# A chunked delta-rule stage: the state update taken over all 128 rows, the output products set directly behind it, and like weight shapes set side by side at the end of a pair

## The chip, the cores and the metric

The kernel is one launch on one core of a Trainium2 chip. The metric is the device time of that launch in microseconds (us). The program is deterministic in what it issues: each engine has its own instruction queue, written out by hand, and the queues meet only in semaphores.

## The reference, cut to what matters

Four layers follow each other on 8 sequences of 512 rows of width 256: attention, a feed-forward layer with 4-bit weights, a gated delta rule, and a feed-forward layer with ternary weights. The change is in the third. Its core is a scan over chunks of 64 rows, with a 128x128 state S for each head (8 heads, 8 chunks in a sequence):

```python
def step(S, inp):
    q_i, k_i, v_i, kc_i, g_i, dm_i = inp
    attn = jnp.where(keep_low, q_i @ jnp.swapaxes(k_i, -1, -2) * dm_i, 0.0)
    v_n = v_i - kc_i @ S
    out = q_i * jnp.exp(g_i)[..., None] @ S + attn @ v_n
    g_last = g_i[..., -1]
    S = S * jnp.exp(g_last)[..., None, None] + jnp.einsum('bhck,bhcv->bhkv',
            k_i * jnp.exp(g_last[..., None] - g_i)[..., None], v_n)
    return (S, out)
```

Ahead of the scan each head needs its projections (q, k, v and an output gate z from one weight matrix), a convolution of four taps, norms, and the inverse of a 64x64 triangular matrix for each chunk (`solve_triangular`). All of it is in float32.

## The kernel before, in words

`delta_rule` is the third stage, between 1061 and some 2940 us of the profiled execution. It works on pairs of heads: 8 sequences of 4 pairs make `PAIRS` = 32 pairs, and `e` is 0 or 1 for the head in the pair. A tile `t` is 128 rows of the sequence (`TPS` = 4) and holds `CPT` = 2 chunks of `CK` = 64 rows; a chunk `m` (`NCH` = 8) has `t = m // 2`, `c = m % 2`, and lies in the partitions `rows(c)`, which are 0 to 63 or 64 to 127.

Every engine runs `for q in range(-1, PAIRS)` with two pairs in hand: the scan of pair `q` (the back) and the projections, taps and norms of pair `f = q + 1` (the front). The first part of a turn is a loop over `n` from 0 to 8, in which step `n` of the scan is mixed with pieces of the front (`front_early(f, n)`, `front_late(f, n)`) in an order written by hand. Then come `LEVELS` - 1 = 5 levels of the triangular inverse for pair `f` and, last, products that prepare its scan. I call the loop over `n` the loop, and the products after the levels the end of the pair.

A step `n` of the scan is a chain between TensorE (PE) and VectorE (DVE), for both heads one after the other:

- PE, line 1966: one product of `PQ` with the state `S` gives k_cum times S and q times S (`p1_mm`)
- DVE, line 1743: `V2`, the new values of the chunk, 64 partitions (`w_done`); ScalarE (ACT), line 1493: the half of the output that comes from S (`o1_done`)
- PE, line 1982: the state update, `KK` transposed times `V2`, over the 64 partitions of the chunk (`ds_mm`)
- DVE, line 1759: `S` is scaled and the update is added (`s_done`), after which PE can start step n + 1

At every odd `n` a tile is complete: PE forms the output products `AT` times `V2` (line 1997, four matmuls, each over 64 partitions and into 64 partitions; `oi_mm`), and DVE adds them to `O` (line 1771, `o_done`). DVE's queue in a step is: V2, a piece of the front (`front_early`), the S updates, at odd `n` the O updates, another piece of the front (`front_late`).

Other names in what follows: line 1844 is the projection of the gate (`gate_in`), 1828 those of keys, values and queries, 1861 and 1876 transposes and Gram products of the keys, 1896 a transpose of the triangular matrices (`lower_across`), 2008, 2025 and 2030 the levels, 1884 and 1888 the query products, 2051 and 2058 the two products at the end of a pair (`vk_mm`, `kc_mm`). On DVE, line 1555 writes `KE` (`kk_done`), which the value projections wait for, 1559 and 1561 are the norms, 1582 is `lower`, which waits for key scales that GpSimd (POOL) computes in `key_scales` (lines 1323 to 1339) from the norms of both heads (`rk_done`). Line 1595 and 1597 are DVE's part of a level.

A float32 matmul shows in the trace as two MATMUL records, each with a weight load (LDWEIGHTS) of its own. The profile writes the shape of the weights ahead of that of the moving operand: 64*128 is a weight tile on 64 partitions (rows of the array) and 128 columns.

Of the kernel before, what the change touches and what calls it, by code (L numbers as in the profile page):

```python
# [21 lines left out]
P = 128  # L22
B, N, D = 8, 512, 256
TPS = N // P
# [15 lines left out]
class Stage:  # L40
# [8 lines left out]
    def sb(self, name, shape, dt=F32):  # L49
        return self.ctx.enter_context(self.nc.sbuf_tensor(f"{self.name}_{name}", shape, dt))  # L50
# [4 lines left out]
    def sem(self, name):  # L55
        handle = self.nc.alloc_semaphore(name=f"{self.name}_{name}")
        self.sems.append(handle)
        return handle
# [876 lines left out]
def delta_rule(nc, sems, X, C, prep, ffn, W_qkvz, W_ba, conv_w, dt_bias, A_log, norm_weight, W_out):  # L935
# [10 lines left out]
    H, DK, CK = 8, P, 64  # L946
# [8 lines left out]
    with ExitStack() as ctx:  # L955
# [222 lines left out]
        AT = [[sb(f"AT{e}{i}", [P, TPS, CK]) for i in range(2)] for e in E2]  # L1178
        KE, VV = [sb(f"KE{e}", [P, TPS, DK]) for e in E2], [sb(f"VV{e}", [P, TPS, DK]) for e in E2]
        NTm, U, L, ZS = ([sb(f"{n}{e}", [P, TPS, CK]) for e in E2] for n in ("NT", "U", "L", "ZS"))  # L1180
        V2, O = [sb(f"V2{e}", [P, TPS, DK]) for e in E2], [sb(f"O{e}", [P, TPS, DK]) for e in E2]
        S = [sb(f"S{e}", [P, DK]) for e in E2]
        ssk, ssq, rk, rq, cc, rkinv, ra, fac, ms, t8 = (
            sb(n, [P, 2, TPS]) for n in ("ssk", "ssq", "rk", "rq", "cc", "rkinv", "ra", "fac", "ms", "t8"))
# [7 lines left out]
        def per_head(*names):  # L1192
# [12 lines left out]
        gb_in = [[sem(f"gb_in{e}{i}") for i in range(2)] for e in E2]  # L1205
        rk_step, rk_done, rq_step, rq_done, fac_step, fac_done = (
            sem(n) for n in ("rk_step", "rk_done", "rq_step", "rq_done", "fac_step", "fac_done"))
        xt_mm, xt_act, xt_dve, op_mm, y_done, st_done, mv_done, eps_done, rstd_done, ln_done = (
            sem(n) for n in ("xt_mm", "xt_act", "xt_dve", "op_mm", "y_done", "st_done", "mv_done", "eps_done", "rstd_done", "ln_done"))

        w_fc, w_proj = ffn
        rawf, rawp, scf, scp, rsf, rsp = ternary_weights(prep, w_fc.shape[0])
# [43 lines left out]
        def rows(c):  # L1256
            return slice(c * CK, (c + 1) * CK)
# [8 lines left out]
        with nc.Block() as block:  # L1266
# [263 lines left out]
            def _(dve):  # L1530
# [199 lines left out]

                dve.wait_ge(xt_mm, DC)
                nc.vector.tensor_copy(xT[:, 1, :], B_[1][:, :]).then_inc(xt_dve, 1)
                for q in range(-1, PAIRS):
                    f = q + 1
                    for n in range(NCH + 1):
                        for e in E2:
                            m = n
                            if has(q) and 1 <= m < NCH:
                                c, t = m % CPT, m // CPT
                                dve.wait_ge(p1_mm[e], q * RS + m)  # L1740
                                if m == 1:
                                    dve.wait_ge(vnc_done[e], q + 1)
                                nc.vector.scalar_tensor_tensor(V2[e][rows(c), t, :], A_[e][rows(c), 0:DK], cneg[q % 2][rows(c), e, t:t + 1],  # L1743
                                                               VV[e][rows(c), t, :], ALU.mult, ALU.add).then_inc(w_done[e], 1)
                        if has(f):
                            front_early(f, n)
# [72 lines left out]
            def _(pe):  # L1819
# [139 lines left out]
                for q in range(-1, PAIRS):  # L1959
                    f = q + 1  # L1960
                    for n in range(NCH + 1):
# [8 lines left out]
                        for e in E2:  # L1970
                            m = n
                            if has(q) and 0 <= m < NCH:
                                c, t = m % CPT, m // CPT
                                if m == 0:
                                    pe.wait_ge(vnc_done[e], q + 1)
                                    pe.wait_ge(kc_done[e], q + 1)
                                    moving = VV[e][rows(c), t, :]
                                else:
                                    pe.wait_ge(w_done[e], q * RS + m)
                                    pe.wait_ge(o1_done[e], q * RS + m)  # L1980
                                    moving = V2[e][rows(c), t, :]
                                nc.tensor.matmul(A_[e][:, DK:2 * DK], KK[e][q % 2][rows(c), t, :], moving, start=True, stop=True).then_inc(ds_mm[e], 1)  # L1982
                        if has(f):
                            front_late(f, n)
                        for e in E2:
                            m = n
                            if has(q) and 0 <= m < NCH and m % CPT == CPT - 1:
                                t = m // CPT
                                if t == 0:
                                    pe.wait_ge(at_done[e], q + 1)  # L1990
                                    if ends_seq(q - 1):
                                        pe.wait_ge(y_done, (seq(q - 1) + 1) * TPS)
                                else:
                                    pe.wait_ge(o_done[e], q * TPS + t)
                                for c in range(CPT):
                                    source = VV if t == 0 and c == 0 else V2
                                    last = nc.tensor.matmul(B_[e][rows(c), 0:DK], AT[e][q % 2][rows(c), t, :], source[e][rows(c), t, :],  # L1997
                                                            start=True, stop=True)
                                last.then_inc(oi_mm[e], 1)
                    for l in range(1, LEVELS):  # L2000
                        for e in E2:
                            if has(f):
# [40 lines left out]
                    if has(f):  # L2043
                        query_gram(f, 0)
                        query_gram(f, 1)
                        for e in E2:
                            pe.wait_ge(u_done[e], f * LEVELS + LEVELS)
                            pe.wait_ge(vv_done[e], f + 1)
                            for t in range(TPS):
                                for c in range(CPT):  # L2050
                                    last = nc.tensor.matmul(F0[e][rows(c), t * P:(t + 1) * P], U[e][rows(c), t, :], VV[e][rows(c), t, :],
                                                            start=True, stop=True)
                            last.then_inc(vk_mm[e], 1)
                            pe.wait_ge(at_done[e], f + 1)
                            pe.wait_ge(ssq_done[e], f + 1)
                            for t in range(TPS):
# [337 lines left out]
```

## Time and profile before

| | |
|---|---|
| median of 3 runs | 3196.33 us (3190.98 to 3197.37) |
| profiled execution | 3194.53 us |
| its span, first to last instruction | 3192.8 us |
| TensorE busy in the span | 2971.4 us, 93% |
| VectorE busy | 2307.4 us, 72% |
| ScalarE busy | 1235.1 us, 39% |
| GpSimd busy | 1020.7 us, 32% |
| mean granted TensorE clock | 0.965 of full |

The profile is that of one execution. A duration is an instruction's own, and neighbours on an engine overlap, so the cost of a block in its engine's queue is read as the distance from its start to the start of the next block. The state update of n = 0 (line 1982 with `VV`) marks the pairs: the first starts at 1061.35 us, and two that follow are 55.7 us apart in the ordinary case.

### The profile page before, as it was taken

The page shows a single profiled execution, that of the slowest core. Times are in us where ns is not written, and L with a number is a line of the kernel's source. Part 1 is how long each engine was busy: PE and PEld are TensorE (multiplying, and loading weights), DVE is VectorE, ACT ScalarE, POOL GpSimd, SP SyncE. Part 2 cuts the span into 40 slices and gives each one's busy share as a digit, 9 for nine tenths or more (in the row PEclk, how much of TensorE's full clock was granted, in tenths as well). Part 3 has the DMA queues.
Part 4 walks back from the last instruction along what each step waited for, and adds up shares of the span by engine and source line. Part 5 has one row for each costly group of instructions (what it writes and reads, how often), then busy time and mean ns, then how long its engine had stood idle before and what let it go on. Part 6 is the DMA issues. An engine that isn't in the chain of part 4 may idle for free. (4 is left out here: it accounts for less than half of the span.)

```text
span 3192.8 us, 82005 instructions
## 1 busy us (share of the span) xinstructions
PE 2971.4 (93%) x33019; PEld 2051.3 (64%) x33019; DVE 2307.4 (72%) x5231; ACT 1235.1 (39%) x2975; POOL 1020.7 (32%) x1495
## 2 busy tenths in 40 slices
PE   6999999679997999999999999999999999999897
PEld 3444444246663777777777777777777777777565
DVE  4666677878874788688678678678678678676566
ACT  2433333323334344344344344344344344342354
POOL 3555455527772222222222222132132132121011
PEclk8999999789997999999999999999999999998899
DMA  2121111000001111001001001001001001000000
GB/s 83 36 58 31 32 31 34 22 1 1 1 1 47 32 41 32 22 19 32 22 18 32 21 19 32 19 21 32 19 21 32 19 22 32 18 18 2 4 25 27
DMA packets 94040, 80.43 MB, mean 25 GB/s; under 512 B 54992, under 2 KB 68320, under 8 KB 93664
## 3 DMA queue, kind: packets, MB, share of 16 engines
q1 hardware_dynamic: 93664, 75.18, 8.7%
q8 instruction: 264, 4.33, 0.6%
q14 instruction: 112, 0.92, 0.1%
HBM read 57.70 MB, written 4.85 MB: 20 GB/s over the span
## 5 line engine op out<-in xcount | busy, mean ns | idle before, releaser
L1828 PE MATMUL gd_bk<-gd_xT,gd_wh 128*128 128x512 f32 x768 | 397.3, 627 | 8.9 <-DVE gd_KE L1555 7.4
L480 DVE TENSOR_REDUCE at_nm<-at_ring 128x2 f32<-128x256 f32 (+3 forms) x256 | 199.2, 821 | 142.9 <-PE at_ring L623 142.9
L1537 DVE SCALAR_TENSOR_TENSOR gd_YK<-gd_bk,gd_cw,gd_YK 128x511 f32<-128x511 f32 (+2 forms) x384 | 283.1, 743 | 11.8 <-ACT gd_YK L1406 6.1
L1506 ACT COPY gd_ZS<-gd_bk 128x256 f32<-128x256 f32 x320 | 119.1, 372 | 318.3 <-PE gd_bk L2008 312.3
L2008 PE MATMUL gd_bk<-gd_L,gd_NT 64*64 64x64 f32 x5120 | 203.7, 223 | 26.5 <-DVE gd_L L1597 25.9
L2008 PEld LDWEIGHTS gd_bk<-gd_L,gd_NT 64*64 64x64 f32 x5120 | 169.2, 134 | 78.8 <-DVE gd_L L1597 40.2
L1595 DVE COPY_PREDICATED gd_U<-gd_mU,gd_bk 128x256 f32<-128x256 int32 x320 | 141.0, 442 | 105.5 <-PE gd_bk L2030 75.1
L1493 ACT COPY gd_O<-gd_bk 64x128 f32<-64x128 f32 x448 | 108.5, 259 | 274.8 <-PE gd_bk L1966 273.9
L2025 PE MATMUL gd_bk<-gd_U,gd_ZS 64*64 64x64 f32 x5120 | 207.6, 220 | 0.1
L302 POOL TENSOR_TENSOR at_PT<-at_PT,at_dm 128x1024 f32<-128x1024 f32 (+3 forms) x128 | 197.8, 1545 | 10.6
L2025 PEld LDWEIGHTS gd_bk<-gd_U,gd_ZS 64*64 64x64 f32 x5120 | 174.6, 135 | 40.8 <-issue 37.1
L1828 PEld LDWEIGHTS gd_bk<-gd_xT,gd_wh 128*128 128x128 f32 x768 | 127.5, 192 | 97.6 <-issue 66.1
L1982 PE MATMUL gd_bk<-gd_V,gd_KK 64*128 64x128 f32 x896 | 167.2, 308 | 20.9 <-DVE gd_V L1743 17.8
L561 PE MATMUL at_ring<-at_QT,at_KT 32*128 32x512 f32 (+3 forms) x1024 | 168.7, 504 | 17.6 <-DVE at_PT L452 12.8
L1982 PEld LDWEIGHTS gd_bk<-gd_V,gd_KK 64*128 64x128 f32 x896 | 123.5, 189 | 94.3 <-DVE gd_V L1743 77.5
L2030 PE MATMUL gd_bk<-gd_ZS,gd_U 64*64 64x64 f32 x4096 | 162.0, 218 | 0.0
L1966 PEld LDWEIGHTS gd_bk<-gd_S,gd_PQ 128*128 128x128 f32 x896 | 127.7, 195 | 52.2 <-issue 37.2
L1966 PE MATMUL gd_bk<-gd_S,gd_PQ 128*128 128x128 f32 x896 | 159.4, 302 | 0.0
L336 ACT ACTIVATE at_PT<-at_ring 128x1024 f32<-128x1024 f32 (+3 forms) x128 | 90.1, 704 | 178.7 <-PE at_ring L561 178.7
L1316 POOL TENSOR_TENSOR gd_zz<-gd_zz,gd_nw_row 128x512 f32<-128x512 f32 x64 | 81.3, 1270 | 240.1 <-ACT gd_zz L1426 240.1
L1771 DVE SCALAR_TENSOR_TENSOR gd_O<-gd_O,gd_tab,gd_bk 128x128 f32<-128x128 f32 x256 | 78.2, 344 | 105.8 <-PE gd_bk L1997 105.1
L1743 DVE SCALAR_TENSOR_TENSOR gd_V<-gd_bk,gd_cneg,gd_VV 64x128 f32<-64x128 f32 x448 | 138.0, 346 | 18.4 <-PE gd_bk L1966 15.0
(354 smaller groups left out, 6772.0 us busy)
## 6 DMA issues: line engine op xcount, KB each, us to landing
gd_wh<-in_L_attn_W_qkvz SPq DMA_DIRECT2D x64, 512.0 KB, 3.7
gd_gb<-gates SPq DMA_DIRECT2D x128, 64.0 KB, 3.3
X<-in_L_attn_x SPq DMA_DIRECT2D x8, 512.0 KB, 8.7
at_QT<-at_QS SPq DMA_DIRECT2D x128, 32.0 KB, 2.0
at_KT<-at_KS SPq DMA_DIRECT2D x128, 32.0 KB, 2.0
at_OC<-at_Ob SPq DMA_DIRECT2D x128, 32.0 KB, 2.0
at_RC<-inverse SPq DMA_DIRECT2D x128, 32.0 KB, 1.8
out_x<-X SPq DMA_DIRECT2D x8, 512.0 KB, 2.9
```

The lines of the kernel that those rows point to most:

```text
L302: nc.gpsimd.tensor_tensor(PT[s % RP][:, 2:GH, 0:n], PT[s % RP][:, 2:GH, 0:n], dm[:, 0:n].unsqueeze(1).broadcast_to([P, 2, n]), ALU.mult).t ...
L480: nc.vector.tensor_reduce(nm[v % 2][:, k, c0:c0 + HS + 1:HS], set_of(s, 2 + p)[:, :, 0:n], AX.X, ALU.max).then_inc(max_done, 1)
L561: last_ = nc.tensor.matmul(set_of(s, p)[:, i, 0:n], KT[lane(u)][r, k * P:(k + 1) * P], QT[lane(u)][r, k * P:W], start=True, stop=True)
L1537: nc.vector.scalar_tensor_tensor(out[:, s:W], bank_[:, 0:W - s], cw[:, j, head(f, e), CONVK - 1 - s:CONVK - s], out[:, s:W], ALU.mult, ALU ...
L1595: last = nc.vector.copy_predicated(U[e][:, :, :], wide(mU[l]), chunks(A_[e], 1))
L1743: nc.vector.scalar_tensor_tensor(V2[e][rows(c), t, :], A_[e][rows(c), 0:DK], cneg[q % 2][rows(c), e, t:t + 1], VV[e][rows(c), t, :], ALU.m ...
L1828: ins = nc.tensor.matmul(out[:, :], wh[e][:, k, col * DK:(col + 1) * DK], xT[:, k, :], start=k == 0, stop=k == DC - 1)
L1966: nc.tensor.matmul(A_[e][:, 0:DK], PQ[e][q % 2][:, m // CPT, m % CPT, :, :].rearrange("p s n -> p (s n)"), S[e][:, :], start=True, stop=Tr ...
L1982: nc.tensor.matmul(A_[e][:, DK:2 * DK], KK[e][q % 2][rows(c), t, :], moving, start=True, stop=True).then_inc(ds_mm[e], 1)
L2008: last = nc.tensor.matmul(A_[e][rows(c), t * CK:(t + 1) * CK], NTm[e][rows(c), t, :], L[e][rows(c), t, :], start=True, stop=True)
L2025: last = nc.tensor.matmul(A_[e][rows(c), (TPS + t) * CK:(TPS + t + 1) * CK], ZS[e][rows(c), t, :], U[e][rows(c), t, :], start=True, stop=True)
L2030: last = nc.tensor.matmul(A_[e][rows(c), t * CK:(t + 1) * CK], U[e][rows(c), t, :], ZS[e][rows(c), t, :], start=True, stop=True)
```

## The change

`V2` gets a place for each chunk of a tile over all 128 partitions (`[P, 2, CPT, DK]`, two tiles in turn), whose other half is zeroed once by four memsets at the stage's start. The state update then takes all 128 rows of `KK` and of `V2`; the rows of the other chunk meet zeros. Only the update of n = 0, whose values come from `VV`, stays at 64 rows. On PE the output products move ahead of `front_late`, directly behind the state update. At the end of a pair, the products of lines 2051 and 2058 are issued by kind, not by head.

```diff
-        V2, O = [sb(f"V2{e}", [P, TPS, DK]) for e in E2], [sb(f"O{e}", [P, TPS, DK]) for e in E2]
+        V2, O = [sb(f"V2{e}", [P, 2, CPT, DK]) for e in E2], [sb(f"O{e}", [P, TPS, DK]) for e in E2]
...
+                for e in E2:
+                    for c in range(CPT):
+                        last = nc.vector.memset(V2[e][rows(1 - c), :, c, :], 0.0)
+                last.then_inc(v2_clear, 1)
...
-                                nc.vector.scalar_tensor_tensor(V2[e][rows(c), t, :], A_[e][rows(c), 0:DK], cneg[q % 2][rows(c), e, t:t + 1],
+                                nc.vector.scalar_tensor_tensor(V2[e][rows(c), t % 2, c, :], A_[e][rows(c), 0:DK], cneg[q % 2][rows(c), e, t:t + 1],
                                                                VV[e][rows(c), t, :], ALU.mult, ALU.add).then_inc(w_done[e], 1)
...
                                 if m == 0:
                                     pe.wait_ge(vnc_done[e], q + 1)
                                     pe.wait_ge(kc_done[e], q + 1)
-                                    moving = VV[e][rows(c), t, :]
+                                    fixed, moving = KK[e][q % 2][rows(c), t, :], VV[e][rows(c), t, :]
                                 else:
                                     pe.wait_ge(w_done[e], q * RS + m)
                                     pe.wait_ge(o1_done[e], q * RS + m)
-                                    moving = V2[e][rows(c), t, :]
-                                nc.tensor.matmul(A_[e][:, DK:2 * DK], KK[e][q % 2][rows(c), t, :], moving, start=True, stop=True).then_inc(ds_mm[e], 1)
-                        if has(f):
-                            front_late(f, n)
+                                    if q == 0 and m == 1:
+                                        pe.wait_ge(v2_clear, 1)
+                                    fixed, moving = KK[e][q % 2][:, t, :], V2[e][:, t % 2, c, :]
+                                nc.tensor.matmul(A_[e][:, DK:2 * DK], fixed, moving, start=True, stop=True).then_inc(ds_mm[e], 1)
                         for e in E2:
                             m = n
                             if has(q) and 0 <= m < NCH and m % CPT == CPT - 1:
...
                                 for c in range(CPT):
-                                    source = VV if t == 0 and c == 0 else V2
-                                    last = nc.tensor.matmul(B_[e][rows(c), 0:DK], AT[e][q % 2][rows(c), t, :], source[e][rows(c), t, :],
+                                    moving = VV[e][rows(c), t, :] if t == 0 and c == 0 else V2[e][rows(c), t % 2, c, :]
+                                    last = nc.tensor.matmul(B_[e][rows(c), 0:DK], AT[e][q % 2][rows(c), t, :], moving,
                                                             start=True, stop=True)
                                 last.then_inc(oi_mm[e], 1)
+                        if has(f):
+                            front_late(f, n)
...
                             last.then_inc(vk_mm[e], 1)
+                        for e in E2:
                             pe.wait_ge(at_done[e], f + 1)
                             pe.wait_ge(ssq_done[e], f + 1)
```

How PE's queue moves in the loop, steps n = 3 and n = 4 of the first pair that has both a back and a front (`gd_KK` is the state update's weight tile, `gd_AT` that of the output products). Before:

```order
L1966 MATMUL gd_bk<-gd_S,gd_PQ 128x128 x2
L1844 MATMUL gd_bk<-gd_wh,gd_xT 128x128 x4
L1982 MATMUL gd_bk<-gd_V,gd_KK 128x128 x2
L1876 MATMUL gd_bk<-gd_kT 64x64 x8
L1861 MATMUL gd_bk<-ident,gd_kT 128x128 x4
L1997 MATMUL gd_bk<-gd_V,gd_AT 64x128 x4
L1966 MATMUL gd_bk<-gd_S,gd_PQ 128x128 x2
L1876 MATMUL gd_bk<-gd_kT 64x64 x8
L1982 MATMUL gd_bk<-gd_V,gd_KK 128x128 x2
L1828 MATMUL gd_bk<-gd_xT,gd_wh 128x512
```

The same stretch of PE's queue in the changed kernel (its line numbers are 4 to 7 higher):

```order
L1970 MATMUL gd_bk<-gd_S,gd_PQ 128x128 x2
L1848 MATMUL gd_bk<-gd_wh,gd_xT 128x128 x4
L1988 MATMUL gd_bk<-gd_V,gd_KK 128x128 x2
L2001 MATMUL gd_bk<-gd_V,gd_AT 64x128 x4
L1880 MATMUL gd_bk<-gd_kT 64x64 x8
L1865 MATMUL gd_bk<-ident,gd_kT 128x128 x4
L1970 MATMUL gd_bk<-gd_S,gd_PQ 128x128 x2
L1880 MATMUL gd_bk<-gd_kT 64x64 x8
L1988 MATMUL gd_bk<-gd_V,gd_KK 128x128 x2
L1832 MATMUL gd_bk<-gd_xT,gd_wh 128x512
```

The four output products have moved from behind the two blocks of `front_late` to directly behind the state update; the shapes of the state update's output are as before, and its 64 or 128 rows don't show in this view.

PE's queue at the end of a pair, from the second head's query products to the first products of the next turn. Before:

```order
L1888 MATMUL gd_bk<-gd_PQ,gd_kT 64x64 x8
L2051 MATMUL gd_bk<-gd_VV,gd_U 64x128 x8
L2058 MATMUL gd_bk<-gd_U,gd_KE 128x64 x8
L2051 MATMUL gd_bk<-gd_VV,gd_U 64x128 x8
L2058 MATMUL gd_bk<-gd_U,gd_KE 128x64 x8
L1828 MATMUL gd_bk<-gd_xT,gd_wh 128x512 x2
```

The same place in the changed kernel:

```order
L1892 MATMUL gd_bk<-gd_PQ,gd_kT 64x64 x8
L2057 MATMUL gd_bk<-gd_VV,gd_U 64x128 x16
L2065 MATMUL gd_bk<-gd_U,gd_KE 128x64 x16
L1832 MATMUL gd_bk<-gd_xT,gd_wh 128x512 x2
L1988 MATMUL gd_bk<-gd_VV,gd_KK 128x128 x2
```

The second head's value products now stand ahead of the first head's key products.

## Rows read from the trace of the kernel before

**Rows 1.** The page: busy time of each engine, share of the span, instructions
```profile
PE 2971.4 (93%) x33019; PEld 2051.3 (64%) x33019; DVE 2307.4 (72%) x5231; ACT 1235.1 (39%) x2975; POOL 1020.7 (32%) x1495
```

**Rows 2.** Stretches: us; busy PE, PEld, DVE, ACT, POOL; PE clock, DMA, GB/s
```profile
1117.07:1172.78 55.71, 54.33 (x813) 41.52 (x812) 44.05 (x112) 24.02 (x65) 14.19 (x29) 1.00 0.16 47
...
1119.53:1142.70 23.17, 22.62 (x201) 16.83 (x199) 19.05 (x57) 13.14 (x38) 5.25 (x9) 1.00 0.02 5
2036.40:2043.01 6.61, 4.55 (x22) 2.22 (x20) 4.95 (x17) 3.17 (x6) 3.92 (x9) 0.88 0.00 0
```

**Rows 3.** Waits from 1061 to 2911 us: total us, times, longest
```profile
PE gd_bk L2008 <- DVE gd_L L1597: 25.1, 90, 0.3
PE gd_bk L1982 <- DVE gd_V L1743: 17.8, 31, 1.8
PE gd_bk L1828 <- DVE gd_KE L1555: 7.1, 30, 0.2
...
DVE gd_O L1771 <- PE gd_bk L1997: 104.3, 93, 2.3
```

**Rows 4.** Timeline of weight loads, n = 1: start, us from first to last
```profile
1119.86 0.97 PEld L1844 LDWEIGHTS gd_bk<-gd_wh,gd_xT 128*128 128x128 f32 x8
1120.95 0.52 PEld L1982 LDWEIGHTS gd_bk<-gd_V,gd_KK 64*128 64x128 f32 x4
```

**Rows 5.** Timeline of PE's matmuls, n = 1 to the start of n = 3
```profile
1119.53 0.61 PE L1966 MATMUL gd_bk<-gd_S,gd_PQ 128*128 128x128 f32 x4
1119.97 1.06 PE L1844 MATMUL gd_bk<-gd_wh,gd_xT 128*128 128x128 f32 x8
1120.96 0.71 PE L1982 MATMUL gd_bk<-gd_V,gd_KK 64*128 64x128 f32 x4
1121.60 1.16 PE L1844 MATMUL gd_bk<-gd_wh,gd_xT 128*128 128x128 f32 x8
1122.68 0.32 PE L1997 MATMUL gd_bk<-gd_VV,gd_AT 64*64 64x128 f32 x1
...
1123.27 0.71 PE L1966 MATMUL gd_bk<-gd_S,gd_PQ 128*128 128x128 f32 x4
...
1125.93 0.72 PE L1966 MATMUL gd_bk<-gd_S,gd_PQ 128*128 128x128 f32 x4
```

**Rows 6.** Timeline of PE's matmuls, n = 4, n = 5, and the loop's end
```profile
1130.54 0.69 PE L1876 MATMUL gd_bk<-gd_kT 128*64 128x64 f32 x16
1131.31 0.74 PE L1982 MATMUL gd_bk<-gd_V,gd_KK 64*128 64x128 f32 x4
...
1132.95 0.61 PE L1966 MATMUL gd_bk<-gd_S,gd_PQ 128*128 128x128 f32 x4
1133.39 1.02 PE L1828 MATMUL gd_bk<-gd_xT,gd_wh 128*128 128x512 f32 x2
1134.63 0.76 PE L1982 MATMUL gd_bk<-gd_V,gd_KK 64*128 64x128 f32 x4 [0.21 <-DVE gd_V L1743]
...
1142.70 1.98 PE L1828 MATMUL gd_bk<-gd_xT,gd_wh 128*128 128x512 f32 x4
```

**Rows 7.** Timeline of DVE, n = 3 to 5
```profile
1129.80 0.61 DVE L1771 SCALAR_TENSOR_TENSOR gd_O<-gd_O,gd_tab,gd_bk 128x128 f32<-128x128 f32 x2 [1.13 <-PE gd_bk L1997]
...
1130.92 0.59 DVE L1743 SCALAR_TENSOR_TENSOR gd_V<-gd_bk,gd_cneg,gd_VV 64x128 f32<-64x128 f32 x2
...
1133.18 0.42 DVE L1561 TENSOR_REDUCE gd_ssk<-gd_DG 128x4 f32<-128x256 f32 x1
...
1134.22 0.63 DVE L1743 SCALAR_TENSOR_TENSOR gd_V<-gd_bk,gd_cneg,gd_VV 64x128 f32<-64x128 f32 x2
```

**Rows 8.** Timeline of POOL: the last step of the key scales
```profile
1136.54 0.20 POOL L1339 TENSOR_SCALAR gd_cneg<-gd_cc 128x8 f32<-128x8 f32 x1
```

**Rows 9.** Timeline of PE at the end of a pair
```profile
1167.77 1.11 PE L2058 MATMUL gd_bk<-gd_U,gd_KE 64*128 64x64 f32 x16
1168.81 1.09 PE L2051 MATMUL gd_bk<-gd_VV,gd_U 64*64 64x128 f32 x16
```

More of the change, by code:

```diff
@@ L1207, in delta_rule @@
             sem(n) for n in ("rk_step", "rk_done", "rq_step", "rq_done", "fac_step", "fac_done"))
-        xt_mm, xt_act, xt_dve, op_mm, y_done, st_done, mv_done, eps_done, rstd_done, ln_done = (
-            sem(n) for n in ("xt_mm", "xt_act", "xt_dve", "op_mm", "y_done", "st_done", "mv_done", "eps_done", "rstd_done", "ln_done"))
+        xt_mm, xt_act, xt_dve, op_mm, y_done, st_done, mv_done, eps_done, rstd_done, ln_done, v2_clear = (
+            sem(n) for n in ("xt_mm", "xt_act", "xt_dve", "op_mm", "y_done", "st_done", "mv_done", "eps_done", "rstd_done", "ln_done", "v2_clear"))
         w_fc, w_proj = ffn
```

## The prediction

> **What bounds the kernel now.** I read the page first: PE is busy for 93% of the span, DVE for 72% [rows 1]. A busy PE is not yet a bound, so I went to the third stage, where the change lies, and read an ordinary pair of heads as a stretch: 54.33 us of 55.71 are busy on PE, 44.05 on DVE, at the full clock [rows 2]. The waits say the same from the other side: over all pairs PE stood 25.1, 17.8 and 7.1 us for DVE, while DVE stood 104.3 us before its O updates alone, for PE's output products [rows 3]. So PE's own queue sets the stage, nearly gapless, and what a block takes there counts one for one.
>
> Then the timeline, for what the time inside this queue is. Compare blocks of like size in step n = 1 [rows 5]. Line 1966, four records on 128*128 weights between neighbours of the same shape, takes 0.44 us from its start to the next block (1119.53 to 1119.97). The state update, also four records of 128 columns but on 64*128 weights between 128*128 blocks, takes 0.64 (1120.96 to 1121.60). The eight gate records take 0.99 after a block of their own shape and 1.08 (1121.60 to 1122.68) after the state update. The weight loads show why [rows 4]: those of line 1844 begin at 1119.86, 0.11 ahead of their first matmul, so under the block before; those of the state update begin at 1120.95, with their matmul. Where the weight shape changes, nothing is loaded ahead and the block before runs out first. I price a change of shape at 0.64 - 0.44 = **0.20 us**: some 0.1 on either side of the boundary.
>
> **The change, part by part.**
>
> Boundaries in the loop. In each step I count the places in PE's queue where the shape changes, up to the next step's line 1966, before and after: n = 1: 4 and 2; n = 2: 2 and 0; n = 3: 5 and 3; n = 4: 3 and 2; n = 5: 4 and 2; n = 6: 3 and 2; n = 7: 4 and 4 (the state update stands between two 64-row blocks). Steps 0 and 8 stay. The state update itself keeps its four records of 128 columns: its four loads take 0.52 us from first to last and the eight of a 128*128 gate block 0.97, which is (0.97 - 0.52) / 4 = 0.11 us for each further one at either height [rows 4], so 128 rows cost no more than 64. That makes 10 boundaries fewer, 2.0 us a pair. A loop with both a back and a front runs 31 times: 62 us.
>
> A rule speaks against this step. The Trainium skill, in TensorEngine Tiling (Array Packing), section Key Properties, has different tiles of the array load and multiply in parallel, and 64x128 as a mode of two tiles, which full-row products give up. By it four state records side by side would take 0.2 us less than four full ones, and the sum would be smaller by 7 x 0.2 x 31 = 43 us. This trace disagrees, for a reason of this kernel: both heads of a step lie in the same half, and their loads follow one after the other, at the 0.11 us of full-row blocks [rows 4].
>
> Waits in the loop. Here I laid the changed queue out for one pair, from the starts and distances of the ordinary pair: a block of PE keeps its length, less 0.1 us for each side on which the shape no longer changes, and DVE and ACT start when what they wait for is there and their own queue is done. What moves up most is DVE. Its O updates waited 1.13 us at n = 3 [rows 7] because the products stood behind `front_late`; now these stand behind the state update, pass in 0.59 us (1122.68 to 1123.27 [rows 5]), and DVE has the S updates to do meanwhile, so this wait goes. Behind it stood V2 of n = 4, which came only at 1130.92, so that PE's state update began at 1131.31, 0.77 us after the block before it, which needs about 0.61 [rows 6, 7]. That 0.16 goes, and so does the 0.2 before the value projection that waited for KE (7.1 us in 30 waits [rows 3]). At n = 5 the wait for V2 stays: V2 starts at 1134.22, which is 1.27 us after line 1966 at 1132.95, and the update 0.41 later [rows 6, 7]. DVE's five front pieces of n = 4 don't shrink, and in my layout V2 comes at 1.30 and the update at 1.71, where PE is ready at 1.31: a wait of 0.4. One wait is new. `lower` at n = 5 needs POOL's key scales, which are done at 1136.74 [rows 8], 3.56 us after the last norm began at 1133.18 [rows 7]. In the layout DVE comes to it 0.3 us too early, and PE loses some 0.1 us by it at the end of n = 6.
>
> Step by step, before and after, from line 1966 to line 1966: n = 1: 3.74 (1119.53 to 1123.27) and 3.42 (0.44 for line 1966, 0.88 gate, 0.53 update, 0.59 outputs, 0.98 gate); n = 2: 2.66 (to 1125.93) and 2.16 (0.44, 0.88, 0.44, 0.40 transposes) [rows 5]; n = 3 and 4: 7.02 (to 1132.95) and 6.10; n = 5 to 7: 9.75 (to 1142.70 [rows 6]) and 8.83, with the 0.4 and the 0.1 in it. The loop's 23.17 us become 20.5: 2.66 less, 2.0 of it boundaries and **0.6** waits, 19 us over 31 pairs. The bounds: nothing from the waits, or all that I find PE waiting in the loop, about 1.0 a pair (31 us).
>
> The end of a pair. Two boundaries go (before: into 2051, 2058, 2051, 2058 and out; after: two fewer). Here pairs of products use both halves: eight output records pass in 0.59 us [rows 5], 0.43 of it at 0.054 each, if the rest is the boundary; by that pitch the sixteen of line 2058 want 0.86 and take 1.04 (1167.77 to 1168.81 [rows 9]), so 0.18 a boundary. I take 0.16: 0.32 a pair, in 32 pairs, 10 us. The first head's key products now come a block later, but what ACT makes of them is needed only after the keys' projection of the next turn, and DVE's products with the second head's new values come earlier. No wait is added: the norms they wait for are done before the second head's value block ends.
>
> The levels stay as they are: their 25.1 us of waits [rows 3] hang on PE's and DVE's work within a level. The four memsets run once on DVE while it waits for the stage's first projections; two V2 records of 128 columns take 0.63 us [rows 7], so four memsets of twice the width cost at most 2.5 us if that cover were gone. I take 0. The last pair has no front: PE waits there at every step, and I give it nothing.
>
> The sum: 62 + 19 + 10 = **91 us**. The profiled execution took 3194.5; the median is 1.8 above. 3196.3 - 91 = 3105.
>
> **The rivals.**
>
> *Boundaries alone.* If the freed waits come back elsewhere, the time is 3196 - 72 = 3124. For it: DVE is the next engine, and from n = 4 to n = 6 my layout has hardly a gap in either queue.
>
> *All waits go.* If DVE keeps ahead everywhere, 62 + 31 + 10 = 103 give 3093. Against it: V2 of n = 5 is bound by DVE's own queue.
>
> *DVE and POOL take over.* If DVE's loop can't be shortened as laid out (the wait for the key scales grows, or its 19.05 us busy in the loop [rows 2], in which 20.5 leave 1.4 us for every hand-over, don't pack so tightly), only half of the loop's gain is left: 31 x 1.3 + 10 = 50, so 3146.
>
> *The change doesn't do it.* If the 0.20 hangs not on the shape but on the semaphore before the state update, the full-row update pays it too, and only the moved outputs and the pair's end count: about 15 us, 3181. Against it: line 1966 waits for DVE as well and takes 0.44 when its neighbours are like it [rows 5].
>
> *Tiles side by side lose.* With the 43 us of the page's rule, 91 - 43 = 48, so 3148. The trace bears it out nowhere.
>
> *Slower.* The clock. Where PE stood 1.8 us for V2 of n = 5 (a first pair of a sequence), the stretch behind shows 0.88 of the clock [rows 2], at two levels of 1.2 and 2.4 GHz that is 24% of 6.6 us at the lower one. A PE that gets through its blocks sooner waits in more places. A microsecond at half clock loses half a microsecond of work, so 91 us are lost when 182 us more of the stage run at 1.2 GHz, 5.9 in each of 31 pairs; with 7 in each, 109 would be lost and the time be 3214. Against it: in ordinary pairs the clock stays at 1.00 with waits of up to 0.3 us [rows 2, 3], and my longest after is 0.4.
>
> **How the numbers follow.** Likeliest 0.55 (own range 3095 to 3115); boundaries alone 0.14; all waits 0.09; DVE and POOL 0.13; doesn't do it 0.03; tiles 0.02; slower 0.04. The range runs from 3085, below the case of all waits, to 3145, through the middle of the takeover; outside lie half of that case, the last three and the tails of the rest, just under 0.2. About 0.2% (6.4 us) is what a measurement of this kernel can tell from no change. Faster by more than that: 0.95, which is every case but the clock's, less 0.01 for an effect too weak to be told; within it 0.02, with 0.01 from the clock case; slower 0.03.
>
> **What would show it.** The state update with four records on 128*128 at 0.44 us at n = 2, its loads ahead of its matmuls; 0.64 there would be the fourth rival. DVE's waits for the output products near 0 instead of 104.3 us. The ordinary pair at 52.7 us instead of 55.71, its loop at 20.5. A new wait of `lower` for POOL around 0.3 us; if it is over 1 us, or V2 of n = 5 later than 1.3 us behind line 1966, DVE and POOL have taken over. The prediction is wrong if the 0.1 on each side of a boundary isn't given back by a block that has to wait for its semaphore: a waiting block can't load ahead either.

## The result and the profile after

The changed kernel takes 3098.23 us (median of 4 runs, 3096.33 to 3098.95), the kernel before 3193.65 us in the runs beside it: a ratio of 0.9701, 95% interval 0.9684 to 0.9717. That is 95 us less, of which 91 were forecast.

The page of the changed kernel, busy times of the engines, beside [rows 1]:

```profile
span 3096.1 us, 82009 instructions
...
PE 2888.2 (93%) x33019; PEld 2032.0 (66%) x33019; DVE 2308.6 (75%) x5235; ACT 1231.9 (40%) x2975; POOL 1019.9 (33%) x1495
```

PE issues as many instructions as before and is busy 83 us less, DVE does the same work in a shorter span, and PE is still the fullest engine. The ordinary pair as a stretch, which answers to the first row of [rows 2] (us; busy PE, PEld, DVE, ACT, POOL; PE clock, DMA, GB/s):

```profile
1114.95:1167.89 52.94, 52.00 (x814) 41.15 (x813) 44.10 (x112) 23.92 (x65) 14.25 (x29) 1.00 0.17 50
```

It is 2.77 us shorter. The four pairs of a sequence differ in length (before: 57.38 or more, 55.72, 56.75 and 69.86 us), but each of the four kinds is shorter by 2.79 to 2.84 us where the clock is full, so 31 pairs make 86 us. The waits between 1061 and 2815 us, beside [rows 3]:

```profile
PE gd_bk L2014 <- DVE gd_L L1597: 24.9, 91, 0.3
PE gd_bk L1988 <- DVE gd_V L1747: 12.2, 8, 1.7
...
DVE gd_S L1757 <- PE gd_bk L1988: 100.1, 31, 3.6
...
DVE gd_NT L1582 <- POOL gd_cneg L1339: 4.1, 24, 0.2
```

DVE's 104.3 us of waits for the output products are gone, PE's 7.1 us for KE too, and the wait of `lower` for POOL's key scales is new, as forecast. What remains of PE's wait for V2 in this view are eight cases, seven of them, of 1.71 us each, in the first pair of a sequence. Last the timeline of PE for n = 1 and 2, which answers to [rows 5] (line 1970 is 1966, 1848 is 1844, 1988 is 1982, 1865 is 1861, 2001 is 1997):

```profile
1117.41 0.61 PE L1970 MATMUL gd_bk<-gd_S,gd_PQ 128*128 128x128 f32 x4
1117.86 1.06 PE L1848 MATMUL gd_bk<-gd_wh,gd_xT 128*128 128x128 f32 x8
1118.75 0.66 PE L1988 MATMUL gd_bk<-gd_V,gd_KK 128*128 128x128 f32 x4
1119.34 0.32 PE L2001 MATMUL gd_bk<-gd_VV,gd_AT 64*64 64x128 f32 x1
1119.35 0.32 PE L2001 MATMUL gd_bk<-gd_V,gd_AT 64*64 64x128 f32 x1
...
1119.93 1.16 PE L1848 MATMUL gd_bk<-gd_wh,gd_xT 128*128 128x128 f32 x8
1120.92 0.61 PE L1970 MATMUL gd_bk<-gd_S,gd_PQ 128*128 128x128 f32 x4
1121.37 1.06 PE L1848 MATMUL gd_bk<-gd_wh,gd_xT 128*128 128x128 f32 x8
1122.26 0.61 PE L1988 MATMUL gd_bk<-gd_V,gd_KK 128*128 128x128 f32 x4
1122.71 0.60 PE L1865 MATMUL gd_bk<-ident,gd_kT 128*128 128x128 f32 x4
1123.14 0.69 PE L1970 MATMUL gd_bk<-gd_S,gd_PQ 128*128 128x128 f32 x4
```

Read the starts. The gate block after a block of its own shape and ahead of one takes 0.89 us (1117.86 to 1118.75), where it took 0.99; the state update at n = 2 takes 0.45 (1122.26 to 1122.71), where it took 0.64. And its weight loads, in the timeline of loads, begin at 1122.15, 0.11 ahead of its first matmul, as those of its neighbours do:

```profile
1121.26 0.97 PEld L1848 LDWEIGHTS gd_bk<-gd_wh,gd_xT 128*128 128x128 f32 x8
1122.15 0.53 PEld L1988 LDWEIGHTS gd_bk<-gd_V,gd_KK 128*128 128x128 f32 x4
1122.60 0.47 PEld L1865 LDWEIGHTS gd_bk<-ident,gd_kT 128*128 128x128 f32 x4
```

### The profile page after: what moved, and what is told of

It reads as the page before. It is cut to its first block and busy times, and to the rows that moved or that the text cites. A ratio compares the mean times of both kernels' runs of the same rounds, so it can differ in the third digit from the quotient of the medians.

```text
span 3096.1 us, 82009 instructions
## 1 busy us (share of the span) xinstructions
PE 2888.2 (93%) x33019; PEld 2032.0 (66%) x33019; DVE 2308.6 (75%) x5235; ACT 1231.9 (40%) x2975; POOL 1019.9 (33%) x1495
## 5 line engine op out<-in xcount | busy, mean ns | idle before, releaser
L1832 PE MATMUL gd_bk<-gd_xT,gd_wh 128*128 128x512 f32 x768 | 390.2, 618 | 1.8 <-DVE gd_xT L1732 0.9
L1988 PE MATMUL gd_bk<-gd_V,gd_KK 128*128 128x128 f32 x896 | 151.0, 291 | 15.3 <-DVE gd_V L1747 12.9
L1988 PEld LDWEIGHTS gd_bk<-gd_V,gd_KK 128*128 128x128 f32 x896 | 121.8, 191 | 61.9 <-DVE gd_V L1747 54.3
L299 POOL TENSOR_SCALAR_AFFINE_SELECT at_PT<-at_PT 128x256 f32<-128x256 f32 x128 | 54.1, 423 | 297.4 <-ACT at_PT L336 296.8
L338 ACT ACTIVATE at_PT<-at_PT 128x1024 f32<-128x1024 f32 (+3 forms) x128 | 94.3, 737 | 138.9 <-DVE at_PT L452 138.7
```

Source lines behind the costliest of these rows:

```text
L1832: ins = nc.tensor.matmul(out[:, :], wh[e][:, k, col * DK:(col + 1) * DK], xT[:, k, :], start=k == 0, stop=k == DC - 1)
L1988: nc.tensor.matmul(A_[e][:, DK:2 * DK], fixed, moving, start=True, stop=True).then_inc(ds_mm[e], 1)
```

## The experiments

Twelve further kernels, three of them with the whole change undone but for one part. I read each by its time and by the length of its ordinary pair in the trace (before: 55.72 us; changed kernel: 52.93), since that length repeats to 0.02 us in nearly all pairs of its kind, while the time of a launch moves by some 12 us in the kernel before (3185 to 3197). One source of that is known: the stretch from the state update of n = 0 in the last pair to the end of the program takes 276.0 to 287.2 us in the fourteen traces, at a mean clock of 0.93 to 0.86, and not by what the kernel does there: it takes 277.6 us in the changed kernel and 284.1 in stats_early, which issues the same instructions from that point on. So differences of a few us between times say little.

### One part of the change at a time

**rows_only**: the change's V2 and state update, with the queue order of before.

```diff
-                                nc.tensor.matmul(A_[e][:, DK:2 * DK], KK[e][q % 2][rows(c), t, :], moving, start=True, stop=True).then_inc(ds_mm[e], 1)
+                                    fixed, moving = KK[e][q % 2][:, t, :], V2[e][:, t % 2, c, :]
+                                nc.tensor.matmul(A_[e][:, DK:2 * DK], fixed, moving, start=True, stop=True).then_inc(ds_mm[e], 1)
```

> The kernel before with the full-row state update alone (padded V2, 128 rows of KK); outputs behind front_late and the end of the pair as before. Theory 1 (each change of weight shape costs 0.20 us in PE's queue): 9 boundaries fewer in a pair of the loop (n = 1: 4 to 2, n = 2: 2 to 0, n = 3: 5 to 4, n = 4: 3 to 2, n = 5: 4 to 2, n = 6: 3 to 2), so 1.8 us a pair: the ordinary pair 53.9 us, 56 us less in all, near 3138. Theory 2 (the gain comes from DVE no longer waiting for the output products, and the row count is worth nothing): the pair stays at 55.7, near 3194. Theory 3 (the price hangs on the semaphore wait before the state update): as theory 2, and the update's block stays at 0.64 us.

Measured: 3178.75 us, ratio 0.9955 (0.9935 to 0.9975), 15 us less; the pair 55.19, so 0.53 us less and not 1.8. (Over 31 pairs 0.53 makes 16 us.) None of the three theories as I had put them. The blocks did give their 0.2 back: the state update of n = 4 takes 0.59 us, the value projection behind it 0.86 (it was 0.96). But look at n = 5 on PE:

```profile
1127.59 0.61 PE L1970 MATMUL gd_bk<-gd_S,gd_PQ 128*128 128x128 f32 x4
1128.03 1.02 PE L1832 MATMUL gd_bk<-gd_xT,gd_wh 128*128 128x512 f32 x2
1129.46 0.76 PE L1988 MATMUL gd_bk<-gd_V,gd_KK 128*128 128x128 f32 x4 [0.40 <-DVE gd_V L1747]
1130.45 1.13 PE L1832 MATMUL gd_bk<-gd_xT,gd_wh 128*128 128x512 f32 x2 [0.23 <-DVE gd_KE L1555]
```

Two records of 512 columns are done in 0.86, and here 1.43 pass to the state update: what PE saved in the steps before, it waits here for V2. In all pairs these waits are 24.0 us by the profile (17.8 before), and DVE still stands 94.6 us for the output products. Either the late products hold DVE, or DVE's own work fills the loop; **rows_dve_late** below decides.

**order_only**: the kernel before with its `front_late` behind the output products.

```diff
-                        if has(f):
-                            front_late(f, n)
                         for e in E2:
                             m = n
                             if has(q) and 0 <= m < NCH and m % CPT == CPT - 1:
...
                                 last.then_inc(oi_mm[e], 1)
+                        if has(f):
+                            front_late(f, n)
```

> The kernel before with the output products moved directly behind the state update, all else as before (64-row update). Theory 1: boundaries 4 to 3 at n = 1, 5 to 4 at n = 3, 4 to 3 at n = 5, so 0.6 us a pair, plus at most the 0.5 us of freed waits: 18 to 35 us less, 3159 to 3176. Theory 2: nearly the whole gain of the loop, 2.5 us a pair, near 3116.

Measured: 3142.92 us, 0.9842 (0.9818 to 0.9867), 51 us less; the pair 54.00, so 1.72 us less. More than theory 1 allowed, less than theory 2. Three boundaries account for 0.6 by their price; the other 1.1 must be freed waits. PE no longer waits for KE or, in an ordinary pair, for V2 by more than a few hundredths: n = 5 took 4.31 us and takes 3.61.

**end_only**: the kernel before with the second `for e in E2:` between the products of lines 2051 and 2058.

> The kernel before with the products at the end of a pair issued by kind, all else as before. Theory 1: two boundaries fewer, 0.31 us in each of 32 pairs, 10 us less, near 3184; DVE's second new-values product starts about 0.9 us sooner. Rival: the first head's key products come later, and ACT's copies of them hold up the next pair's start: 0 or slower.

Measured: 3182.33 us, 0.9973 (0.9962 to 0.9984), 11 us less; the pair 55.42, 0.30 less. As theory 1 has it.

The three parts alone give 15 + 51 + 11 = 77 us, together 95: in the pair 0.53 + 1.72 + 0.30 = 2.55 and 2.79.

### What a boundary costs by itself

**extra_boundary**: the changed kernel with two blocks of n = 3 swapped.

```diff
                     if n == 3:
-                        key_gram(f, 0)
                         keys_across(f, 1)
+                        key_gram(f, 0)
```

> The changed kernel with two neighbouring blocks of step n = 3 swapped on PE (the second head's key transposes, 128*128, ahead of the first head's Gram products, 128*64, where they stood behind them next to the 128*128 block of line 1970). The same instructions, one change of shape more in a pair. Theory 1: the pair 0.2 us longer, 6 us over 31 pairs, near 3104. Theory 3 (the price hangs on semaphore waits, not on shapes): the pair stays at 52.93, near 3098.

Measured: 3110.02 us, 0.9743 (0.9723 to 0.9763); the pair 53.13, 0.20 longer. By time it is 12 us over the changed kernel, of which the ordinary pairs make 6, two first pairs, at 56.4 us where the other five take 54.74, another 3, and the last stretch, at 280.2 us for 277.6, the rest. In PE's timeline the order is now 64*64, 128*128, 128*64, 128*128:

```profile
1124.31 0.65 PE L2001 MATMUL gd_bk<-gd_V,gd_AT 64*64 64x128 f32 x8
1124.89 0.66 PE L1865 MATMUL gd_bk<-ident,gd_kT 128*128 128x128 f32 x4
1125.48 0.69 PE L1880 MATMUL gd_bk<-gd_kT 128*64 128x64 f32 x16
1126.10 0.71 PE L1970 MATMUL gd_bk<-gd_S,gd_PQ 128*128 128x128 f32 x4
1126.74 0.69 PE L1880 MATMUL gd_bk<-gd_kT 128*64 128x64 f32 x16
```

The transposes take 0.59 instead of 0.49 and line 1970 behind takes 0.64 instead of 0.54: 0.1 on either side, with no wait added. 128*64 against 128*128 is a change of shape like the others.

**n0_full**: the changed kernel with the state update of n = 0 over 128 rows too.

```diff
                     dve.wait_ge(vk_mm[e], f + 1)
+                    nc.vector.tensor_tensor(V2[e][rows(0), 0, 0, :], F0[e][rows(0), 0:DK], cc[rows(0), e, 0:1].broadcast_to([CK, DK]), ALU.mult)
...
-                                    fixed, moving = KK[e][q % 2][rows(c), t, :], VV[e][rows(c), t, :]
+                                    fixed, moving = KK[e][q % 2][:, t, :], V2[e][:, t % 2, c, :]
```

> The changed kernel with the state update of n = 0 over 128 rows too; DVE writes the first chunk's new values into V2 as well, one 64x128 product more for each head at the end of a pair, where it waits for PE anyway. Theory 1: two boundaries fewer, the update's block 0.44 us instead of 0.64 and line 1832 before it 1.82 instead of 1.92: 0.4 us a pair, 12 us less, near 3086. Rival (DVE's extra products hold up the keys' projection, which waits for the new values): 0 to slower.

Measured: 3088.08 us, 0.967 (0.9653 to 0.9686); most ordinary pairs 52.56, 0.37 less than the changed kernel's 52.93. The update of n = 0 takes 0.45 us and the projection before it 1.82.

### What the late output products did

**rows_dve_late**: rows_only, with DVE's `front_late` ahead of its O updates.

```diff
                         if has(f):
                             front_middle(f, n)
+                            front_late(f, n)
                         for e in E2:
...
-                        if has(f):
-                            front_late(f, n)
                         if n == 4 and ends_seq(q - 1):
```

> rows_only (full-row update, outputs on PE still behind front_late) with one change on DVE: its front piece of a step (front_late) now stands ahead of the O updates, so that DVE has work while it waits for the late output products. In rows_only the pair took 55.19 us, 1.3 more than 9 boundaries at 0.20 allow. Theory: DVE, held 0.9 to 1.1 us at n = 1, 3 and 5 by the late products, hands V2 over late, and PE gives the boundaries back as waits; then the pair falls to 53.4 to 53.9 us here, 40 to 55 us less than rows_only, near 3130. Rival (DVE's own work bounds the loop, or the full-row update doesn't save its 0.20): the pair stays near 55.2, 3178.

Measured: 3136.54 us, 0.9823 (0.9801 to 0.9845), 42 us less than rows_only; the pair 53.94, 1.25 less. PE's queue is the same in both, and DVE has the same instructions. So it was the late products, through DVE's queue, and neither DVE's load nor the price of a shape. The steps from line 1966 to line 1966 (us, read from the starts; the row laid out is that of the prediction):

| kernel | n = 1 | 2 | 3 | 4 | 5 | 6 | 7 | loop |
|---|---|---|---|---|---|---|---|---|
| before | 3.74 | 2.66 | 3.97 | 3.05 | 4.31 | 2.87 | 2.57 | 23.17 |
| rows_only | 3.41 | 2.64 | 3.80 | 2.86 | 4.50 | 2.87 | 2.58 | 22.66 |
| rows_dve_late | 3.40 | 2.33 | 3.74 | 2.67 | 4.21 | 2.56 | 2.49 | 21.40 |
| order_only | 3.64 | 2.57 | 3.76 | 2.76 | 3.61 | 2.65 | 2.48 | 21.47 |
| laid out | 3.42 | 2.16 | 6.10 for 3 and 4 | | 8.83 for 5 to 7 | | | 20.51 |
| changed kernel | 3.51 | 2.22 | 3.66 | 2.56 | 3.81 | 2.45 | 2.48 | 20.69 |

### What bounds the changed loop

**no_kk1**: the changed kernel without one DVE piece at n = 4.

```diff
                         key_norms(f, 1)
-                        keys_to_state(f, 1)
+                        if f < 2:
+                            keys_to_state(f, 1)
```

> The changed kernel without one DVE instruction a pair: the second head's key scaling for the state (the last DVE piece of n = 4, 0.69 us) is left out from the third pair on, so the state update of that head uses the keys of an earlier pair. If DVE's queue alone makes PE wait at n = 5 (the block before the update takes 1.12 instead of 0.86 us): that wait and the 0.15 in the update's block go, pair 52.5 us, near 3085. If POOL's key scales are the next bound: DVE then waits about 1 us at line 1582, V2 of n = 6 is late, and the pair falls by 0.1 to 0.2 only, near 3093.

Measured: 3096.74 us, 0.9698 (0.9678 to 0.9717); the pair 52.95, no shorter at all. The step n = 5 fell from 3.81 to 3.39 us, as DVE's theory has it, and n = 6 rose from 2.45 to 2.78, n = 7 from 2.48 to 2.58. DVE's timeline at n = 5 shows what took over:

```profile
1130.46 0.60 DVE L1776 SCALAR_TENSOR_TENSOR gd_O<-gd_O,gd_tab,gd_bk 128x128 f32<-128x128 f32 x2
1131.82 0.86 DVE L1582 SCALAR_TENSOR_TENSOR gd_NT<-gd_bk,gd_cneg,gd_gb 128x64 f32<-128x64 f32 x4 [0.76 <-POOL gd_cneg L1339]
1132.60 0.59 DVE L1748 SCALAR_TENSOR_TENSOR gd_V<-gd_bk,gd_cneg,gd_VV 64x128 f32<-64x128 f32 x2
```

DVE stands 0.76 us for POOL's key scales with V2 of n = 6 behind it in its queue. I had expected this bound to give back half or more of the gain; with n = 7 it gave back all. The first pairs of a sequence did get shorter, from 54.54 to 53.95 us, as PE's wait for V2 there fell from 1.71 to 1.11 us.

**n0_stats_act**: n0_full and the statistics at n = 0 (below), and ACT's first tap of the second head's keys behind its copies of n = 1.

```diff
                     if n == 0:
                         keys_first(f, 0)
-                        keys_first(f, 1)
                     if n == 1:
+                        keys_first(f, 1)
                         keys_out(f, 0)
```

> n0_stats with ACT's first tap of the second head's keys moved behind its two copies of n = 1. In the changed kernel the first tap ended at 1118.30 and the copies began at 1118.33, while V2 was ready earlier, and the update of n = 1 took 0.59 us where its shape asks for 0.53. If ACT holds it: 0.05 us a pair, under 2 us in all, 3073; too small to tell by time, the block's length in the trace tells it. Rival: nothing changes, or the next tap on DVE comes late and the pair is longer.

Measured: 3072.28 us, 0.962 (0.9601 to 0.964), against 3074.70 for n0_stats, which by time is no difference; the update of n = 1 takes 0.54 us instead of 0.59 and the pair 52.51 instead of 52.56. So ACT held that update, by 0.05 us.

**dve_later**: n0_stats_act with the key scaling and both `lower` one place later on DVE.

```diff
                     if n == 5:
+                        keys_to_state(f, 1)
                         keys_to_inverse(f, 1)
                     if n == 6:
-                        lower(f, 1)
+                        lower(f, 0)
...
                         key_norms(f, 1)
-                        keys_to_state(f, 1)
-                    if n == 5:
-                        lower(f, 0)
                     if n == 6:
-                        values_tap(f, 0, 1)
+                        lower(f, 1)
                     if n == 8:
+                        values_tap(f, 0, 1)
```

> n0_stats_act with DVE's front pieces of the loop put one place later each, for both bounds that no_kk1 showed: the second head's key scaling moves from the end of n = 4 to n = 5 ahead of KE, lower of the first head to the start of n = 6 (behind V2, where POOL's key scales are long done), lower of the second to the end of n = 6, the first value tap to n = 8. Theory (n = 5 waits for DVE's queue, and taking only that away moves the wait to POOL's scales at n = 6; with both eased it is gone): n = 5 from 3.8 to 3.4 us and n = 6 stays near 2.5, the pair from 52.5 to 52.1, 12 us less, near 3060. Rival (the later lower makes PE's lower products of n = 7 or the first level wait): the pair at 52.5 or above.

Measured: 3070.12 us, 0.9609 (0.959 to 0.9627); against n0_stats_act (0.962, 0.9601 to 0.964) the intervals overlap. The ordinary pair is 52.30, 0.21 less and not 0.4. n = 5 fell to 3.55 and not 3.4, since PE's projection now waits for KE, which has the key scaling ahead of it; and the first pairs of a sequence grew from 52.55 to between 52.96 and 53.20, with the longest wait of the levels for DVE at 0.9 us where it was 0.3. Half of the gain is given back in places that had no slack for one more DVE piece.

### The first pair of a sequence

**stats_early**: the changed kernel with one DVE block moved. **stats_early_before**: the same move in the kernel before.

```diff
+                        if n == 0 and ends_seq(q - 1):
+                            statistics(seq(q - 1))
                         if has(f):
                             front_early(f, n)
...
-                        if n == 4 and ends_seq(q - 1):
-                            statistics(seq(q - 1))
```

> The changed kernel with DVE's statistics of the last sequence moved from n = 4 of the first pair of a sequence to n = 0, where DVE stands 3.56 us for PE. If the 1.6 us by which these 7 pairs are longer than the ordinary (54.54 against 52.93) are PE waiting for V2 behind the statistics: all 7 go to 52.9, 11 us less, near 3087. Rival (the extra lies in the DVE work wherever it stands, or in the normalisation at n = 8): 54.5 stays, near 3098.

Measured: 3090.09 us, 0.9676 (0.9659 to 0.9693); the seven first pairs take 53.0 us instead of 54.54. PE's waits for V2 over all pairs fell from 12.2 to 0.2 us, which is the view of waits of this kernel:

```profile
PE gd_bk L2014 <- DVE gd_L L1597: 25.9, 93, 0.3
PE gd_bk L1988 <- DVE gd_V L1747: 0.2, 1, 0.2
```

> The kernel before with the same move of the statistics. There the first pairs took 57.38 (3 of them), 58.70 (3) and 59.94 (1) against 55.72. Theory: the wait of 1.8 us costs 1.66 by itself, and in four of the seven the granted clock fell after it (0.97 and 0.94 mean in the pair), for 1.3 to 2.6 us more; without the wait there is no fall, so 18 us less, near 3175: more than the 11 us in the changed kernel. Rival (the fall of the clock has nothing to do with this wait): 12 us less, near 3182, with 0.97 still in some pairs.

Measured: 3171.39 us, 0.9936 (0.9915 to 0.9956), 20 us less by the ratio; all seven first pairs take 55.8 us at a clock of 1.00, which is 17.8 us less in the sum of the seven, as the theory has it and not the rival. The windows of the fifth pair of the stage in the kernel before, of the ninth, and of the ninth in this kernel (there from line 1966 of n = 1 to the next):

```profile
1299.38:1356.76 57.38, 54.40 (x813) 41.54 (x813) 47.66 (x126) 24.03 (x65) 15.42 (x31) 1.00 0.09 25
...
1539.28:1597.97 58.69, 55.76 (x813) 42.31 (x813) 47.83 (x126) 24.04 (x65) 15.54 (x31) 0.97 0.09 25
```

```profile
1539.01:1594.79 55.78, 54.40 (x814) 41.54 (x812) 45.95 (x119) 24.05 (x65) 15.45 (x30) 1.00 0.09 26
```

The first two rows are the first pairs of two sequences, with the same instructions and the same wait of 1.82 us, and take 57.38 and 58.69 us. The difference is in PE's busy time (54.40 and 55.76) and goes with the clock, and it is gone where the wait is.

**n0_stats**: n0_full and stats_early together.

> Both: the state update of n = 0 over 128 rows and the statistics at n = 0. If they don't touch, the gains add: 12 + 11 = 23 us less than the changed kernel, near 3075. Rival: both use DVE's wait at the start of a pair; if it is too short for both in the first pair of a sequence, some of the 11 us is lost there.

Measured: 3074.70 us, 0.9625 (0.961 to 0.964), 24 us less than the changed kernel. By time the two alone gave 10 and 8; by the ordinary pairs of the one and the first pairs of the other 11 and 11, which is what adds here. In n0_full six of the seven first pairs had grown to 55.8 us, which took some of its gain; here all of them take 52.6, as the ordinary ones.

## Why the prediction was right

**What bounds the kernel.** Right. PE's queue set the stage, and its boundaries could be read one by one. The ordinary pair came to 52.93 for 52.7 forecast.

**The price of a boundary.** Right, and shown by itself: 0.20 us in extra_boundary, where nothing but the order of two blocks differs. n0_full took two away for 0.37. The price hangs on the shape, not on the semaphore: the state update waits for one in every kernel and loads ahead as soon as its neighbours are like it and the semaphore is there in time. Where it really has to wait, at n = 5, it starts its loads with its matmuls (0.69 us at n = 5 of the changed kernel), which is the caution I had closed with.

**The tiles side by side.** By the Trainium skill (TensorEngine Tiling (Array Packing), section Key Properties) different tiles can load and multiply in parallel. The trace agrees where both halves are in use: the output products start in twos, 0.01 us apart (1119.34 and 1119.35). The state update has no second tile to run beside, since both heads lie in the same half, and giving up the 64-row form cost nothing: its four loads take 0.53 us for 0.52, and the block 0.45 for 0.64.

**The waits.** The net was 0.6 us a pair (2.66 - 2.0 is nearer 0.7, which would have made the sum 92 to 93); measured 2.48 - 2.0 = 0.48 in the loop. The steps n = 1 to 4 came out 0.27 us longer than laid out, n = 5 to 7 0.09 shorter. That the waits freed by the move can't exceed 1.0 us a pair was wrong: order_only frees 1.1. V2 of n = 5 came 1.16 us after line 1970 instead of 1.30, `lower` waited 0.17 us for POOL instead of 0.3. I missed ACT at n = 1: its first tap ended at 1118.30 and held the copy that the update waits for; 0.05 us a pair.

**The end of a pair.** 0.30 for 0.32 forecast.

**The sum.** 31 x 2.79 us are 86 of the 95, against 91 forecast. The rest I had not in it, and it isn't shown to be the change's: in the profiled execution of before, four first pairs took 1.3 to 2.6 us more than the three others, at a lower clock, 6.5 us in all, and in the changed kernel none did; the stretch from the state update of n = 0 in the last pair to the end shrank by 3.6 us (281.2 to 277.6), at a clock of 0.92 where it was 0.88. That stretch moves by 11 us from trace to trace whatever the kernel. And the changed kernel has the same wait in its first pairs (1.71 us) as extra_boundary, rows_dve_late and n0_full, in which two, three and six of the seven first pairs were followed into the lower level. So some 10 of the 97 us between the two profiled executions are their clock, which is luck for the total; what the layout was made for fell 5 us short.

**The rivals.** The clock as a rival had a lower level behind PE's waits, and that is what the runs show, but only behind the long wait of the first pairs; the waits of an ordinary pair, 0.3 us at most in the changed kernel, never brought it. The rival that the change doesn't do it was priced too low in its gain: it gave 15 us to the moved outputs and the end of the pair, and these two alone brought 51 and 11, so such a world would have shown some 3134 us and not 3181. What excludes it is the 0.45 us of the state update's block and extra_boundary, not the total.

**Where a reader would go wrong with it.** The sum read as if 2.0 us came from the full rows and the order, and 0.6 from the order alone. The runs show that the parts don't stand alone. Nine of the ten boundaries go with the full rows, 1.8 us, and alone they bring 0.53, since DVE waits for late output products and hands V2 over no sooner. The move of four matmuls, worth 0.6 in boundaries, brings 1.72 alone. After it the full rows bring 0.78 (21.47 to 20.69 in the table) of the 1.4 us that their remaining seven boundaries are worth. Most of what is missing is at n = 5, which has one boundary fewer and yet takes 3.81 us for 3.61, since DVE's queue hands V2 over late; n = 6 gives its 0.2 in full (2.65 to 2.45), so POOL's scales, for which `lower` waits 0.17 us, cost PE nothing yet. That the total came near is owed to the layout, which was made for the whole change at once.

## What to carry to other kernels

Price a queue by the distance from start to start of its blocks, and compare blocks of one size with like and unlike neighbours: that shows what a change of weight shape costs, and whether loads run ahead. Before counting such savings on a full engine, follow what the other queue waits for in each step: an instruction whose result nobody needs soon can still hold, in the queue of the engine that takes it up, the instruction that everybody needs. And when one wait is taken away, look which chain is 0.1 us behind it; here easing DVE's queue alone brought nothing in the ordinary pair, since POOL's scales stood behind it, and easing ACT's copies brought 0.05 us.

## What the runs showed of the hardware

A change of weight shape between neighbouring blocks of matmuls costs 0.2 us at the full clock, 0.1 at the end of the one and 0.1 at the start of the other: for 128*128 against 128*64 by extra_boundary (0.20 for one more), against 64*128 by n0_full (0.37 for two fewer), against 64*64 by line 1970 at n = 7 of the changed kernel, which takes 0.64 us between two blocks of 64*64 (1135.62 to 1136.26) and 0.44 between blocks of its own shape, 0.1 on each side. Between 64*64 and 64*128, with two halves of the array in use, it costs 0.15 (end_only, 0.30 for two fewer). The price is that of a block whose semaphore is there in time; a block that has to wait starts its loads only with its matmuls, whatever stands beside it.

A single wait of 1.5 to 2 us on PE sometimes costs more than itself. In every trace, all time at the lower of the two clock levels between the first pair and the last lies in the first pairs of a sequence, behind PE's wait for V2 of n = 5, and costs 1.3 to 2.6 us on top of the wait where the same kernel has a first pair without it to compare:

| PE's wait in the first pairs | kernels, and first pairs with a stretch at the lower level, of 7 |
|---|---|
| 2.01 us | rows_only 7 |
| 1.82 us | before 4, end_only 2 |
| 1.71 us | changed kernel 0, extra_boundary 2, rows_dve_late 3, n0_full 6 |
| 1.52 us | order_only 3 |
| 1.11 us | no_kk1 0 |
| none of this kind | stats_early, stats_early_before, n0_stats, n0_stats_act, dve_later 0 each |

That is 27 of 56 with the long wait and 0 of 42 without it, so no fall of the clock was seen without it. Why some of the long waits were followed by it and others of the same length not, these runs leave open; each trace is one execution, and the changed kernel's 0 of 7 is no proof that it is free of it.
